# A second layer turned token-major for one half of the tokens, and a shorter head

## The chip, the core and the metric

The kernel runs on one core of a Trainium2 chip. The metric is the time on the device of one execution, in microseconds. The core's engines are TensorE (PE), VectorE (DVE), ScalarE (ACT), GpSimd (POOL) and SyncE (SP, which here only issues DMAs). Each runs its own queue in order; they meet at semaphores.

## What is computed

1024 tokens of 256 features pass two blocks, each with a layer norm ahead of it and a residual behind it. In the first block each token belongs to one of 4 experts by its token id; an expert's gate, up and down matrices are all the same 256 x 256 matrix. The second block is a mixture of 16 experts of 96 features, 4 per token, and a shared expert.

```python
# block 1, for each expert e (Wg, Wu, Wd are all ctx_2048)
g = silu(einsum('bsd,fd->bsf', h, Wg[e]))
u = einsum('bsd,fd->bsf', h, Wu[e])
y = einsum('bsf,df->bsd', g * u, Wd[e])
out = where((expert_ids == e)[..., None], y, out)
# block 2
scores = sigmoid(x @ router_w.T);  top 4 of scores + e_bias, weights normalised
routed = sum_e combine[:, e] * ((silu(g) * u) @ down_e.T)
# around them
x = x + block1(layernorm(x), ids)
x = x + block2(layernorm(x))
```

## The kernel before

The tokens are two halves of 512 (`h` = 0, 1), in tiles of 128. Inside a block the data lie feature-major: 128 features on the partitions, 512 tokens along the row, two such blocks of features (`KC` = 2). Matrices and activations are split into a high part of reduced precision and a low remainder, and each product is three matmuls (high x high, low weight x high, high weight x low), so a 512-column result over 256 features is 6 matmuls.

Block 1 is eight "mixes", written out in `mixes` (L291): (layer, half, feature block). A mix computes its 128 features for all 4 experts into 4 PSUM banks (24 matmuls of 512 columns); ACT copies expert 0 (`first_z`), and DVE overwrites the tokens of experts 1 to 3 with predicated copies (`pick`, masks from `thresholds`). Behind a layer-1 mix ACT takes the silu (`silu_z`), DVE multiplies (`hidden_product`), the high part is cast (`hidden_high` on ACT or `hidden_cast` on DVE), and DVE subtracts for the low part (`hidden_low`). Behind a layer-2 mix DVE adds the residual in `xt` (`add_block_1`), which gives x1. Six PSUM banks form a ring over the mixes (`ring_order`).

The layer norm wants tokens on the partitions. For half 0 of block 2, PE turns x1 (`x1_transposes`, 8 transposes of 128 x 128, in the midst of mix 5), DVE takes the statistics (`tile_stats(2)`, `layer_norm_vars(2)`), POOL the power -0.5 (`rstd_of`), DVE and ACT normalise two tiles each (`layer_norm_apply`, `apply_norm`), and PE turns the result back (`norm_transposes("n2", ...)`, behind the first 12 matmuls of mix 6). For half 1 of block 2 the turning goes over DVE's 32 x 32 transposes and DRAM (`turn_x1`, `write_x1`, `read_x1`, `turn_xn`, `write_xn`, `read_xn`), beside the second block's steps.

At the head, the tokens of half 0 are only centred ahead of the matmuls (tiles 0 and 2 on DVE by `centre`, 1 and 3 on ACT), and the deviation is multiplied in later as a row (`scale`, from `rstd_all`, which goes through DRAM). POOL subtracts for the low parts of the weights (`low_part(n)`, one per piece) and takes the powers. PE starts with 8 warm matmuls on zeros and has one more (256 columns) between the first and second pair of transposes (`first_transposes`).

Block 2 is a list of 26 steps (`items`): gate and up matmuls, then DVE's `product` with the router's weights (a row spread over the partitions by DMA, `spread_rows` on SP), `hidden_2`, a cast on ACT, `hid_low` on DVE, and two steps later the down matmuls.

The orders of all queues are written out by hand at the end of each engine's block: POOL's L480 to L497, ACT's L601 to L653, DVE's L874 to L964, PE's L1159 to L1184, SP's L370 to L454.

Of the kernel before, what the change touches and what calls it, by code (L numbers as in the profile page):

```python
# [61 lines left out]
XN_TURN, XN_WRITE, XN_READ = 6, 10, 11  # L62
SPREADS = 4
# [16 lines left out]
def build(nc, first_d, x_d, xt_d, ids_d, ctx_d, bias_d, gu_d, wd0_d, wd_d, out_d):  # L80
# [4 lines left out]
    with ExitStack() as ctx:  # L85
# [3 lines left out]
        def sem(name):  # L89
# [6 lines left out]
        xt = sb("xt", [P, KC, TOKENS])  # L96
        stage = sb("stage", [P, SLOTS, STAGE])
# [18 lines left out]
        power = sb("power", [P, TT])  # L116
# [27 lines left out]
        x1_d = nc.dram_tensor("x1_d", (HALF, D), F32, kind="Internal").ap()  # L144
        xn_d = nc.dram_tensor("xn_d", (QUARTERS, KC, LANES, HALF), F32, kind="Internal").ap()
# [26 lines left out]
        side_done, first_turned = sem("side_done"), sem("first_turned")  # L172
        xhi_done, xlo_done = sem("xhi_done"), sem("xlo_done")
# [17 lines left out]
                      ("x1", 0, 0, 4), ("x1", 0, 1, 5), ("n2", 0, 0, 4), ("n2", 0, 1, 5)]  # L191
        side_at = {u[:3]: n for n, u in enumerate(side_order)}

        def wait_side_read(eng, b, n):

            before = [u for u in side_order[:n] if u[3] == b]
            if not before:
                eng.wait_ge(pair_low, 1)
                eng.wait_ge(xlo_done, KC)
                return  # L200
            what, h, k, _ = before[-1]
            if what in ("n1", "n2"):
                count = (HALVES * KC if what == "n2" else 0) + h * KC + k + 1
                eng.wait_ge(xhi_done, max(count, KC))
                eng.wait_ge(xlo_done, count)
            else:
                eng.wait_ge(normed_v, (HALVES + 1) * TT // 2)
                eng.wait_ge(normed_a, (HALVES + 1) * TT // 2)

        ring_order = [("z", n, e) for n in range(7) for e in range(E1)]  # L210
        ring_order += [("gate", 0, 0), ("up", 0, 0)] + [("z", 7, e) for e in range(E1)]
# [5 lines left out]
        def wait_ring_read(eng, what, n, e):  # L217
# [7 lines left out]
            elif what == "z":  # L225
                eng.wait_ge(z_picked, n * (E1 - 1) + e)

# [14 lines left out]
        def wait_features(eng, what, h, k):  # L242
# [3 lines left out]
            else:  # L246
                eng.wait_ge(side_done, side_at[what, h, k] + 1)

# [42 lines left out]
        mixes = [(1, 0, 0), (1, 0, 1), (1, 1, 0), (2, 0, 0), (2, 0, 1), (1, 1, 1), (2, 1, 0), (2, 1, 1)]  # L291
        mixed = {mix: n for n, mix in enumerate(mixes)}

        def wait_mixed(eng, n):

            layer, h, m = mixes[n]
            eng.wait_ge(h1_done if layer == 1 else x1_done, h * KC + m + 1)
# [47 lines left out]
        def tile_to_norm(n, t):  # L345

            if n != HALVES:
                return x[:, n % HALVES * TT + t]
            at = t % (TT // KC) * D
            return side_bank("x1", 0, t // (TT // KC))[:, at:at + D]  # L350
# [10 lines left out]
        def _(sp):  # L361
# [15 lines left out]
            sp.dma_start(xt[:], xt_d).then_inc(xt_in, 16)  # L377
# [45 lines left out]

            def spread_rows(g):
# [10 lines left out]
            for g in range(1, N):  # L435
# [13 lines left out]
                if g == XN_READ:  # L449
                    read_xn()  # L450
                if g == place[1, SPREADS]:
# [5 lines left out]
        def _(pool):  # L457
# [16 lines left out]

            def rstd_of(n):

                pool.wait_ge(varied, n + 1)
                nc.gpsimd.tensor_tensor(deviation[:, 0:TT] if n == 0 else rstd[:, n], vareps[:, n], power[:], ALU.pow).then_inc(powered, 1)
# [21 lines left out]
        def _(act):  # L500
# [23 lines left out]

            def centre(t):
# [7 lines left out]
            def apply_norm(n):  # L533
# [4 lines left out]
                else:  # L538
                    act.wait_ge(side_done, side_at[("n1", 1, 1) if n == HALVES else ("n2", 0, 1)] + 1)
                for t in range(TT):  # L540
                    if t not in BY_VECTOR[n]:
                        nc.scalar.activation(xn[:, t], tile_to_norm(n, t), ACT.Identity, bias=shift[:, n, t:t + 1],
                                             scale=rstd[:, n, t:t + 1]).then_inc(normed_a, 1)

            def hidden_high(b):
                act.wait_ge(h1_product, b + 1)
                nc.scalar.activation(h_hi[:, b], hid[:, b % 2], ACT.Copy).then_inc(h1_high, 1)
# [678 lines left out]
```

## Time and profile before

| | us |
|---|---|
| median of 3 runs | 169.66 (169.48 to 169.74) |
| the profiled execution | 169.34 |
| its span in the trace | 167.2 |
| PE busy (share of the span) | 162.5 (97%) |
| DVE busy | 114.5 (68%) |
| ACT busy | 68.7 (41%) |
| POOL busy | 37.2 (22%) |

The span runs from the first to the last recorded event; the rest of the execution's time lies around it. Busy times of PE come from pipelined matmuls, so a matmul's own duration (0.395 us for 512 columns) is longer than the distance from one to the next. The chain of work that ended last is 95% PE: 23% of the span in `mix` (L1030), 41% in the gate and up matmuls, 21% in the down matmuls. A line of the timeline gives start, duration, engine, line, operation, output and inputs, a count where several were merged, and in brackets the idle time before it and what ended that.

### The profile page before, as it was taken

To read this page: it belongs to the slowest core of one execution; us is meant where nothing else is said; L and a number is where in the kernel's file an instruction comes from. 1 tells how busy PE (TensorE), PEld (TensorE's weight loads), DVE (VectorE), ACT (ScalarE), POOL (GpSimd) and SP (SyncE) were. 2 spreads that over 40 slices of the span, in tenths; PEclk is the share of its full clock that TensorE was granted. 3 is DMA by queue.
4 is the path that set the end of the run, shared out by engine and by line. 5 is a ranking of instruction groups with operands and counts; after the bars stand their busy time and mean duration, and the time that the engine had idled before them with its cause. 6 is when DMAs were issued, how large, how long until landed. Compare 5 with 4: busy or idle time off the path is not lost.

```text
span 167.2 us, 2186 instructions
## 1 busy us (share of the span) xinstructions
PE 162.5 (97%) x705; PEld 128.9 (77%) x705; DVE 114.5 (68%) x237; ACT 68.7 (41%) x116; POOL 37.2 (22%) x36
## 2 busy tenths in 40 slices
PE   7999999999999999999999999999999999999992
PEld 2788888888778888888888878888888888888880
DVE  1889999666957998779986744967714444444462
ACT  3654342831359134536734538452222222222210
POOL 1384000656241045556970000000000000000000
PEclk9999999999999999999999999999999999999999
DMA  5891380164304065987225400025441112200003
GB/s 172 275 408 44 107 291 0 21 206 161 115 4 127 16 205 192 219 240 211 67 61 163 153 0 4 1 103 165 173 141 67 63 63 63 65 0 0 4 0 125
DMA packets 12199, 18.78 MB, mean 112 GB/s; under 512 B 3772, under 2 KB 6044, under 8 KB 12060
## 3 DMA queue, kind: packets, MB, share of 16 engines
q1 hardware_dynamic: 12188, 18.64, 34.9%
q8 instruction: 6, 0.10, 0.2%
q14 instruction: 5, 0.04, 0.1%
HBM read 16.39 MB, written 2.24 MB: 111 GB/s over the span
## 4 chain that ended last, share of the span: by engine, by line
PE 95%; DMA 2%; DVE 1%; DVEq 0%; issue 0%
PE bank L1030 23%; PE bank L1131 15%; PE bank L1129 13%; PE bank L1130 13%; PE bank L1149 7%; PE bank L1152 7%; PE bank L1150 7%; DMA first<-first_d 2%; PE bank L998 1%; PE bank L1071 1%; PE bank L1065 1%; PE bank L1126 1%; PE bank L1125 1%; PE bank L987 1%; PE bank L1078 1%; PE bank L1060 1%
## 5 line engine op out<-in xcount | busy, mean ns | idle before, releaser
L1131 PE MATMUL bank<-xn_lo,gu_hi 128*128 128x512 f32 (+1 forms) x104 | 41.1, 395 | 0.0
L1129 PE MATMUL bank<-xn_hi,gu_lo 128*128 128x512 f32 x96 | 38.0, 396 | 0.0
L1130 PE MATMUL bank<-xn_hi,gu_hi 128*128 128x512 f32 x96 | 38.0, 396 | 0.0
L599 ACT ACTIVATE h_hi<-hid 128x512 fp32r<-128x512 f32 (+1 forms) x26 | 16.4, 632 | 45.6 <-DVE hid L860 45.6
L865 DVE TENSOR_TENSOR h_lo<-hid,h_hi 128x512 fp32r<-128x512 f32 (+1 forms) x26 | 18.0, 691 | 14.9 <-ACT h_hi L599 14.9
L1131 PEld LDWEIGHTS bank<-xn_lo,gu_hi 128*128 128x128 f32 (+1 forms) x104 | 19.4, 187 | 4.9
L589 ACT ACTIVATE act_sb<-bank 128x512 f32<-128x512 f32 (+1 forms) x26 | 15.4, 592 | 17.5 <-PE bank L1131 17.4
L472 POOL TENSOR_TENSOR gu_lo<-stage,gu_hi 128x512 fp32r<-128x512 f32 x12 | 17.2, 1457 | 21.7 <-ACT gu_hi L504 16.3
L1129 PEld LDWEIGHTS bank<-xn_hi,gu_lo 128*128 128x128 f32 x96 | 18.0, 188 | 4.4
L1130 PEld LDWEIGHTS bank<-xn_hi,gu_hi 128*128 128x128 f32 x96 | 18.0, 188 | 4.3
L749 DVE COPY_PREDICATED prod<-beyond,bank 128x512 f32<-128x512 uint8 x24 | 17.6, 737 | 5.1 <-PE bank L1030 4.4
L1149 PE MATMUL bank<-h_hi,wd_lo 128*128 128x512 f32 (+1 forms) x52 | 20.6, 396 | 0.0
L1150 PE MATMUL bank<-h_hi,wd_hi 128*128 128x512 f32 (+1 forms) x52 | 20.6, 395 | 0.0
L1152 PE MATMUL bank<-h_lo,wd_hi 128*128 128x512 f32 (+1 forms) x52 | 20.5, 395 | 0.0
L860 DVE TENSOR_TENSOR hid<-prod,bank 128x512 f32<-128x512 f32 x24 | 16.5, 688 | 2.0
L847 DVE TENSOR_TENSOR prod<-act_sb,ids 128x512 f32<-128x512 f32 x12 | 9.6, 796 | 8.6 <-ACT act_sb L589 8.6
L847 DVE TENSOR_TENSOR prod<-act_sb,first 128x512 f32<-128x512 f32 x12 | 10.0, 832 | 6.3 <-ACT act_sb L589 5.7
L1030 PE MATMUL bank<-h_hi,ctx_hi 128*128 128x512 f32 x32 | 12.7, 398 | 0.0
L1030 PE MATMUL bank<-h_lo,ctx_hi 128*128 128x512 f32 x32 | 12.7, 395 | 0.0
L1030 PE MATMUL bank<-h_hi,ctx_lo 128*128 128x512 f32 x32 | 12.7, 395 | 0.0
L1152 PEld LDWEIGHTS bank<-h_lo,wd_hi 128*128 128x128 f32 (+1 forms) x52 | 9.8, 188 | 2.4
L1150 PEld LDWEIGHTS bank<-h_hi,wd_hi 128*128 128x128 f32 (+1 forms) x52 | 9.8, 188 | 2.3
(102 smaller groups left out, 213.2 us busy)
## 6 DMA issues: line engine op xcount, KB each, us to landing
stage<-gu_d SPq DMA_DIRECT2D x6, 512.0 KB, 3.9
stage<-wd_d SPq DMA_DIRECT2D x3, 512.0 KB, 4.3
first<-comb_d SPq DMA_DIRECT2D x8, 192.0 KB, 2.9
ids<-comb_d SPq DMA_DIRECT2D x8, 192.0 KB, 3.3
stage<-ctx_d SPq DMA_DIRECT2D x4, 256.0 KB, 6.0
xt<-xt_d SPq DMA_DIRECT2D x1, 1024.0 KB, 9.9
first<-comb_d SPq DMA_DIRECT2D x8, 128.0 KB, 3.0
ids<-comb_d SPq DMA_DIRECT2D x8, 128.0 KB, 2.9
```

The lines of the kernel that those rows point to most:

```text
L472: ins = nc.gpsimd.tensor_tensor(lo[:, s], st[:, s], hi[:, s].bitcast(F32), ALU.subtract)
L749: nc.vector.copy_predicated(prod[:, n % 2], beyond[:, e - 1, h * HALF:(h + 1) * HALF], ring_bank("z", n, e)[:]).then_inc(z_picked, 1)
L847: nc.vector.tensor_tensor(prod[:, g % 2], act_sb[:, g % 2], rows, ALU.mult).then_inc(prod_done, 1)
L860: nc.vector.tensor_tensor(hid[0:w, g % 2], src, up_bank(g)[0:w, :], ALU.mult).then_inc(hid_done, 1)
L865: nc.vector.tensor_tensor(h_lo[0:w, slot[g]], hid[0:w, g % 2], h_hi[0:w, slot[g]].bitcast(F32), ALU.subtract).then_inc(hlo_done, 1)
L1030: return nc.tensor.matmul(ring_bank("z", n, e)[:], (ctx_hi, ctx_lo)[a][:, m, e, k], parts[k][b], start=start, stop=stop)
L1129: nc.tensor.matmul(out[:], gu_lo[:, cols], xn_hi[:, h, k], start=(k == 0), stop=False)
L1130: nc.tensor.matmul(out[:], gu_hi[:, cols], xn_hi[:, h, k], start=False, stop=False)
L1131: ins = nc.tensor.matmul(out[0:rows, :], gu_hi[:, wide], xn_lo[:, h, k], start=False, stop=(k == KC - 1))
L1149: nc.tensor.matmul(acc[k][:], wd_lo[0:w, c, cols], hi, start=(c == 0), stop=False)
L1150: nc.tensor.matmul(acc[k][:], wd_hi[0:w, c, cols], hi, start=False, stop=False)
L1152: ins = nc.tensor.matmul(acc[k][:], wd_hi[0:w, c, cols], lo, start=False, stop=(c == ITEMS - 1))
```

## The change

- Half 0's second layer is computed with tokens on the partitions (`row_mix`): the stationary operand is a block of 128 tokens of the hidden activations, the moving operand the matrices of a pair of experts, 512 columns. So x1 of half 0 comes out token-major in `x1_rows`. `x1_transposes`, its two entries of `side_order` and the mixes (2, 0, 0) and (2, 0, 1) go; the list of mixes has six entries now, and the order is mixes 0, 1, 2, the rows, 3, 4, 5.
- ACT copies expert 0's columns (`row_z`, 256 per tile), DVE picks experts 1 to 3 in operations of 256 columns with a mask of one byte per token (`row_thresholds`, `pick_rows`), adds the residual (`add_rows`), and takes the statistics from there.
- The tokens of a tile are dealt out in runs of 32 (`hidden` writes them so), and "n2"'s transposes undo that with a strided output.
- x1 of half 0 is needed feature-major for the last residual: DVE's transposes behind steps 8 and 9 (`turn_x0`), DMAs behind 12 and 13 of SP's loop (`write_x0`, `read_x0`), and `output(0)` waits for them.
- POOL waits for the four row adds (instead of x1) ahead of `low_part(7)` and `rstd_of(2)`. `layer_norm_apply(2)` lies ahead of the last pick of mix 3.
- At the head DVE's `centre` sums and subtracts (`tensor_reduce`, `scalar_tensor_tensor`) in place of `bn_stats`, `bn_aggr` and a subtraction; all four tiles' statistics come later. The warm matmul between the pairs goes. One power of 8 columns stands for two of 4, ahead of `low_part(3)` rather than behind it, and waits for the second half's variances.
- The residual is loaded in two halves, half 0 token-major, and the ids of half 0 once more by tokens.

```diff
-        mixes = [(1, 0, 0), (1, 0, 1), (1, 1, 0), (2, 0, 0), (2, 0, 1), (1, 1, 1), (2, 1, 0), (2, 1, 1)]
+        mixes = [(1, 0, 0), (1, 0, 1), (1, 1, 0), (1, 1, 1), (2, 1, 0), (2, 1, 1)]
...
+        def hidden(tile, b, at):
+            if b >= KC:
+                return tile[:, at]
+            order = "p (b t j) -> p b t j" if tile is hid else "p (t b j) -> p b t j"
+            return tile[:, at].rearrange(order, t=TT, j=LANES)
...
+            def first_deviations():
+                pool.wait_ge(varied, HALVES)
+                nc.gpsimd.tensor_tensor(deviation[:, 0:HALVES * TT], vareps[:, 0:HALVES].rearrange("p n t -> p (n t)"),
+                                        power[:], ALU.pow).then_inc(powered, HALVES)
...
-            for n in range(E1):
+            for n in range(E1 - 1):
                 low_part(n)
-            rstd_of(0)
-            rstd_of(1)
+            first_deviations()
+            low_part(E1 - 1)
             for n in range(E1, E1 + 3):
                 low_part(n)
-            pool.wait_ge(x1_done, KC)
+            pool.wait_ge(row_added, TT)
             low_part(E1 + 3)
             rstd_of(2)
...
             first_z(2)
-            first_z(3)
+            row_z(0)
             silu_z(2)
             hidden_high(2)
+            row_z(1)
             high_part(4)
             high_part(5)
+            row_z(2)
             high_part(6)
-            first_z(4)
+            row_z(3)
             high_part(7)
             high_part(8)
             router_low_rows()
-            first_z(5)
-            silu_z(5)
+            first_z(3)
             apply_norm(2)
+            silu_z(3)
...
             def centre(t):
                 dve.wait_ge(x_in[t // (TT // 2)], 16)
-                tile_stats(0, t)
+                step(nc.vector.tensor_reduce(minus_mean[:, t:t + 1], x[:, t], AX.X, ALU.add))
                 dve.wait_ge(dstep, steps[0])
-                step(nc.vector.bn_aggr(meanvar[:, 0, t], stats[:, t]))
-                dve.wait_ge(dstep, steps[0])
-                nc.vector.tensor_scalar(xn[:, t], x[:, t], meanvar[:, 0, t, 0:1], None, ALU.subtract).then_inc(normed_v, 1)
+                nc.vector.scalar_tensor_tensor(out=xn[:, t], in0=minus_mean[:, t:t + 1].to_broadcast([P, D]), scalar=-1.0 / D, in1=x[:, t],
+                                               op0=ALU.mult, op1=ALU.add).then_inc(normed_v, 1)
...
+            def pick_rows(t, experts=range(1, E1)):
+                dve.wait_ge(row_first, t + 1)
+                dve.wait_ge(rows_masked, E1 - 1)
+                for e in experts:
+                    dve.wait_ge(row_done, 2 * t + e // 2 + 1)
+                    if e > 1:
+                        dve.wait_ge(row_picked, t * (E1 - 1) + e - 1)
+                    z = ring_bank("rows", t, e // 2)[:, e % 2 * D:(e % 2 + 1) * D]
+                    nc.vector.copy_predicated(x1_rows[:, t], beyond_rows[:, e - 1, t:t + 1].to_broadcast([P, D]),
+                                              z).then_inc(row_picked, 1)
+            def add_rows(t):
+                dve.wait_ge(row_picked, (t + 1) * (E1 - 1))
+                dve.wait_ge(x_rows_in, 16)
+                residual = xt[:, t * D // HALF, t * D % HALF:][:, 0:D]
+                nc.vector.tensor_tensor(x1_rows[:, t], x1_rows[:, t], residual, ALU.add).then_inc(row_added, 1)
...
             masked.append(thresholds(1))
+            row_thresholds()
             pick(2, masked[1])
-            pick(3, masked[0], [1])
+            pick_rows(0, [1])
             hidden_product(2)
-            pick(3, masked[0], [2])
+            pick_rows(0, [2])
             hidden_low(2)
-            pick(3, masked[0], [3])
-            add_block_1(3)
-            pick(4, masked[0])
+            pick_rows(0, [3])
+            add_rows(0)
+            for t in range(1, TT):
+                tile_stats(2, t - 1)
+                pick_rows(t)
+                add_rows(t)
+            tile_stats(2, TT - 1)
+            layer_norm_vars(2)
+            pick(3, masked[1], [1, 2])
+            layer_norm_apply(2)
+            pick(3, masked[1], [3])
+            hidden_product(3)
+            hidden_cast(3)
+            hidden_low(3)
+            x_low("n2", 0, 0)
+            x_low("n2", 0, 1)
...
-                for t, warm_steps in enumerate((0, 0, 1, 0)):
-                    keep_warm(warm_steps, HALF // 2)
+                for t in range(TT):
                     wait_normed(pe, 0, t)
...
+            def row_mix():
+                hi, lo = ([w[:, b].rearrange("p (t c) -> p t c", c=P) for b in range(KC)] for w in (h_hi, h_lo))
+                def moving(w, pair, k):
+                    return w[:, :, 2 * pair:2 * pair + 2, k].rearrange("p m e f -> p e m f")
+                for t in range(TT):
+                    for pair in range(2):
+                        wait_ring_read(pe, "rows", t, pair)
+                        out = ring_bank("rows", t, pair)[:].rearrange("p (e m f) -> p e m f", e=2, m=KC)
+                        for k in range(KC):
+                            if t == 0 and pair == 0:
+                                pe.wait_ge(h1_high, k + 1)
+                            nc.tensor.matmul(out, hi[k][:, t], moving(ctx_hi, pair, k), start=(k == 0), stop=False)
+                            nc.tensor.matmul(out, hi[k][:, t], moving(ctx_lo, pair, k), start=False, stop=False)
+                            if t == 0 and pair == 0:
+                                pe.wait_ge(h1_done, k + 1)
+                            ins = nc.tensor.matmul(out, lo[k][:, t], moving(ctx_hi, pair, k), start=False, stop=(k == KC - 1))
+                        ins.then_inc(row_done, 1)
...
             mix(1, {1: lambda: norm_transposes("n1", 1, 1)})
-            for n in range(2, 5):
-                mix(n)
-            mix(5, {1: lambda: (x1_transposes(0, 0), x1_transposes(0, 1))})
-            mix(6, features=[0])
+            mix(2)
+            row_mix()
+            mix(3)
+            mix(4, features=[0])
             norm_transposes("n2", 2, 0)
-            mix(6, experts=[0, 1], features=[1])
+            mix(4, experts=[0, 1], features=[1])
             gate_or_up(0, False)
             gate_or_up(0, True)
```

## Rows read from the trace of the kernel before

**Rows 1.** The page, busy time, share of the span and instructions of each engine.
```profile
PE 162.5 (97%) x705; PEld 128.9 (77%) x705; DVE 114.5 (68%) x237; ACT 68.7 (41%) x116; POOL 37.2 (22%) x36
```

**Rows 2.** What PE waited for: us in total, times, longest.
```profile
PE bank L977 <- DVE warm L874: 1.2, 1, 1.2
PE bank L998 <- DVE xn L687: 0.3, 1, 0.3
```

**Rows 3.** The chain that ended last: start (end of the one before), us, work.
```profile
6.12 0.21 PE bank L977
...
16.67 22.39 PE bank L1030 x96
39.06 0.87 PE bank L1010 x8
...
45.53 0.87 PE bank L987 x8
```

**Rows 4.** Timeline of DVE: second variances, first norm, mixes 2 and 5, second block.
```profile
12.50 0.17 DVE L678 TENSOR_SCALAR vareps<-meanvar 128x4 f32<-128x4 f32 x1
...
14.59 0.16 DVE L713 SCALAR_TENSOR_TENSOR shift<-meanvar,rstd 128x4 f32<-128x4 f32 x1
14.67 0.73 DVE L721 TENSOR_SCALAR xn<-first,meanvar,rstd 128x256 f32<-128x256 f32 x2
...
25.56 3.19 DVE L749 COPY_PREDICATED prod<-beyond,bank 128x512 f32<-128x512 uint8 x4
28.69 0.69 DVE L757 TENSOR_TENSOR hid<-act_sb,prod 128x512 f32<-128x512 f32 x1
...
45.09 0.43 DVE L763 TENSOR_SCALAR h_hi<-hid 128x512 fp32r<-128x512 f32 x1
...
60.86 1.61 DVE L847 TENSOR_TENSOR prod<-act_sb,first 128x512 f32<-128x512 f32 x1 [0.18 <-DMA first<-comb_d]
```

**Rows 5.** Groups of DVE by form: busy us, mean ns; idle before, releaser.
```profile
L749 DVE COPY_PREDICATED prod<-beyond,bank 128x512 f32<-128x512 uint8 x24 | 17.6, 737 | 5.1 <-PE bank L1030 4.4
L865 DVE TENSOR_TENSOR h_lo<-hid,h_hi 128x512 fp32r<-128x512 f32 x24 | 16.6, 691 | 14.7 <-ACT h_hi L599 14.7
...
L670 DVE BATCH_NORM_STATS2 stats<-first 128x6 f32<-128x256 f32 x12 | 4.4, 416 | 3.3 <-DMA first<-first_d 2.7 <-DMA first<-x_d 0.5
...
L872 DVE TENSOR_TENSOR xt<-bank,xt 128x256 f32<-128x256 f32 x2 | 0.8, 420 | 0.7 <-PE bank L1152 0.7
```

**Rows 6.** Timeline of ACT: first norm, the cast of mix 2, the first late weights.
```profile
14.79 1.09 ACT L542 ACTIVATE xn<-first,shift,rstd 128x256 f32<-128x256 f32 x2 [4.30 <-DVE shift L713]
...
29.41 0.63 ACT L547 ACTIVATE h_hi<-hid 128x512 fp32r<-128x512 f32 x1 [0.76 <-DVE hid L757]
29.95 1.51 ACT L504 ACTIVATE gu_hi<-stage 128x448 fp32r<-128x448 f32 x2
```

**Rows 7.** Timeline of POOL: a memset, the first powers, low parts of the weights.
```profile
0.73 0.10 POOL L458 MEMSET power<- 128x4 f32 x1 [0.29 <-POOLq L1219]
...
12.55 1.18 POOL L478 TENSOR_TENSOR deviation<-vareps,power 128x4 f32<-128x4 f32 x1
13.53 1.03 POOL L478 TENSOR_TENSOR rstd<-vareps,power 128x4 f32<-128x4 f32 x1
30.59 1.22 POOL L468 TENSOR_TENSOR gu_lo<-stage,gu_hi 128x448 fp32r<-128x448 f32 x1 [16.03 <-ACT gu_hi L504]
31.77 3.05 POOL L472 TENSOR_TENSOR gu_lo<-stage,gu_hi 128x512 fp32r<-128x512 f32 x2
...
37.91 2.54 POOL L472 TENSOR_TENSOR wd_lo<-stage,wd_hi 128x512 fp32r<-128x512 f32 x2 [2.38 <-DVE xt L777]
...
60.63 2.99 POOL L472 TENSOR_TENSOR gu_lo<-stage,gu_hi 128x512 fp32r<-128x512 f32 x2 [9.75 <-ACT gu_hi L504]
```

**Rows 8.** Timeline of PE: the transposes of the two norms.
```profile
15.64 1.03 PE L987 MATMUL bank<-first,xn 128*128 128x128 f32 x8
...
45.37 1.04 PE L987 MATMUL bank<-first,xn 128*128 128x128 f32 x8
```

More of the change, by code:

```diff
@@ L201, in wait_side_read @@
             what, h, k, _ = before[-1]
[L202 to L211, printed above, removed]
+            count = (HALVES * KC if what == "n2" else 0) + h * KC + k + 1
+            eng.wait_ge(xhi_done, max(count, KC))
+            eng.wait_ge(xlo_done, count)
+        ring_order = [("z", n, e) for n in range(3) for e in range(E1)]
+        ring_order += [("rows", t, pair) for t in range(TT) for pair in range(2)]
+        ring_order += [("z", n, e) for n in (3, 4) for e in range(E1)]
+        ring_order += [("gate", 0, 0), ("up", 0, 0)] + [("z", 5, e) for e in range(E1)]
         ring_at = {u: n for n, u in enumerate(ring_order)}
@@ L226, in wait_ring_read @@
                 eng.wait_ge(z_picked, n * (E1 - 1) + e)
+            elif what == "rows" and e == 0:
+                eng.wait_ge(row_first, n + 1)
+                eng.wait_ge(row_picked, n * (E1 - 1) + 1)
+            elif what == "rows":
+                eng.wait_ge(row_picked, (n + 1) * (E1 - 1))
         def side_bank(what, h, c):
@@ L422, in read_xn, with write_x0, read_x0 @@
                     sp.dma_start(xn_turn[q * LANES:(q + 1) * LANES], rows[q]).then_inc(xn_back, 16)
+            def write_x0():
+                sp.wait_ge(x0_turned, TT)
+                rows = turn_d.rearrange("q k i (b c) -> b i (q k) c", c=P)
+                blocks = x[:, TT:].rearrange("p t d -> p (t d)").rearrange("p (m c) -> p m c", c=P)
+                for b in range(QUARTERS):
+                    sp.dma_start(rows[b], blocks[b * LANES:(b + 1) * LANES]).then_inc(x0_out, 16)
+            def read_x0():
+                sp.wait_ge(x0_out, QUARTERS * 16)
+                rows = turn_d.rearrange("q k i n -> q i k n")
+                for q in range(QUARTERS):
+                    sp.dma_start(xt[q * LANES:(q + 1) * LANES, :, 0:HALF], rows[q]).then_inc(x0_back, 16)
             def spread_rows(g):
@@ L450, in _ @@
                     read_xn()
+                if g == X0_WRITE:
+                    write_x0()
+                if g == X0_READ:
+                    read_x0()
                 if g == place[1, SPREADS]:
@@ L523, in first_z, with row_z @@
                 nc.scalar.activation(prod[:, n % 2], ring_bank("z", n, 0)[:], ACT.Copy).then_inc(z_first, 1)
+            def row_z(t):
+                act.wait_ge(row_done, 2 * t + 1)
+                nc.scalar.activation(x1_rows[:, t], ring_bank("rows", t, 0)[:, 0:D], ACT.Copy).then_inc(row_first, 1)
             def centre(t):
@@ L768, in hidden_low @@
                 dve.wait_ge(h1_high, b + 1)
-                nc.vector.tensor_tensor(h_lo[:, b], hid[:, b % 2], h_hi[:, b].bitcast(F32),
+                nc.vector.tensor_tensor(hidden(h_lo, b, b), hidden(hid, b, b % 2), hidden(h_hi, b, b).bitcast(F32),
                                         ALU.subtract).then_inc(h1_done, 1)
```

129 lines of the change are left out of this document (73 added, 56 removed).

## The prediction

> **What bounds the kernel now.** I read the page's busy times first, then what TensorE (PE) waits for, then the chain of work that ended last, and only then the other engines' timelines around the two places that the diff touches. PE is busy for 162.5 of 167.2 us [rows 1], and its waits come to 1.5 us in all, both in the first 5 us [rows 2]. So from there on PE never waits, and the time is PE's own instruction stream. Its pace is read from the chain: 96 matmuls of 512 columns in 22.39 us, 0.233 us each [rows 3]. Two things follow. A PE instruction taken out behind the head gives back its full price. And a new PE wait is paid in full too, since nothing behind it has slack to give back. The question is whether the other engines still deliver in time.
>
> **What PE loses and gains.** `x1_transposes` goes: 8 transposes in 0.87 us [rows 3], so -0.87 us. `row_mix` has 4 token tiles x 2 pairs of experts x 2 feature halves x 3 terms = 48 matmuls of 512 columns; the two mixes that it replaces had 2 x 4 x 2 x 3 = 48. I take the same 0.233 us. Its moving operand is four runs of 128 columns instead of one of 512, and the "n2" transposes write runs of 32; no row shows either. At 2% more on the 48 it would be +0.2 us; a gain is excluded, since as many columns stream. I take 0.
>
> **The new chain behind the rows.** Most of the forecast hangs on it. All times are in the clock of the trace before.
> PE: mix 1 has 12 matmuls left at 16.67 and mix 2 has 24, so the rows start at 16.67 + 36 x 0.233 = 25.07 and end at 25.07 + 11.2 = 36.27; mix 3 (half 1, layer 1, feature 1) ends at 41.87, the first 12 of mix 4 at 44.67, the 8 "n2" transposes at 45.54. That is 0.87 us ahead of before, as it must be (45.53 + 0.87 there [rows 3]). The next matmul needs `h_hi` of mix 3's block, the third needs `h_lo`.
> DVE: 512 elements of a tensor_tensor take 0.69 [rows 4], 256 take 0.42, a pick of 512 takes 0.737 [rows 5]. A pick of 256 is not in the trace; it lies between half of 0.737 (0.37) and 0.737. The step of 0.27 us that separates the two tensor_tensors gives 0.47, and I take that. Four picks in a row take 3.19 us [rows 4], so one that waits for the one before it starts 0.1 us after its end: 0.57 per pick. A tile is three picks (1.71), an add (0.42) and its stats (0.42 [rows 5], of which some 0.07 overlaps): 2.5 us. PE makes one each 2.8 us, so DVE would keep up, but it starts behind. Three thresholds of 4 elements come first (0.1 each, the 0.17 us of such an instruction [rows 4] overlapped), so mix 2's picks start at 25.86 instead of 25.56 and everything behind them is 0.3 us later: product at 28.99 for 28.69, its cast on ScalarE (ACT) at 29.71 for 29.41 [rows 6], `h_lo` 30.41 to 31.08. Tile 0's first two picks fill the gaps in which DVE waits for ACT; the third ends at 31.47 and the add wants to start at 31.57.
> POOL then stands in the way. ACT is 0.3 us later and has one row copy (0.3) ahead of its 448-wide cast, which goes from 29.95 [rows 6] to 30.55. POOL's 1.22 us subtraction came 0.64 us behind that cast's start [rows 7]: now 31.2 to 32.4. An operation of DVE with two inputs in SBUF waits for a POOL operation that runs: the product at 60.86 took 1.61 us instead of 0.69 [rows 4] beside a POOL subtraction that began at 60.63 [rows 7]. So add 0 ends at about 32.7, not 32.0. POOL's two halves of 512 follow, 1.3 us each once DVE lets go, until 35.1; add 1, wanted at 34.76, ends at 35.4. Tiles 2 and 3 have no such company: add 2 ends at 37.9, add 3 at 40.4.
> POOL waits for that last add (`row_added`, 4), and then has `low_part(7)`, 2.54 us [rows 7], and the power, 1.03, in that order: 40.48 + 2.54 + 1.03 = 44.05. (`low_part(7)` began at 37.91 before.) `layer_norm_apply(2)` stands in DVE's queue ahead of the last pick of mix 3. From the power to the end of its two tiles are 0.8 us (14.56 to 15.40 in the other norm [rows 4, 7]), so that pick starts at 44.86, although its matmuls ended at 41.87. Queued behind it is the rest of that block's path: pick 0.74, silu 0.63, product 0.69, cast 0.43, with 0.03 between [rows 4 to 6]: `h_hi` at 47.45, `h_lo` at 48.2. PE had issued its transposes by 45.37 + 0.87 before [rows 8], and has by 45.4 now; it stands until 47.5, 2.2 us, and 0.3 us more at `h_lo`. The new wait is +2.5 us.
> Its bounds: without POOL's company the last add is 1.0 us earlier, and at 0.37 per pick some 11 picks on the path give 1.1: 0.4 us is left. With the variances and a strided cast of layer 1 held up too (0.2 and 0.3 us) it is 3.0.
> The page "VectorE: DVE Perf Modes" of the Trainium skill, section "The TRN2 errata", speaks against just this part: each small operation pays a fixed latency, and it advises 512 elements or more. Its formula for PSUM sources gives 0.39 us for a pick of 256, an estimate; by it the wait would be 0.9 us shorter. For 512 it gives 0.66, below the 0.737 of the row here.
>
> **The head.** Out go a `bn_aggr` on DVE with its wait and one warm matmul (0.21 us [rows 3]) between the pairs. DVE's first tile may come 0.2 us earlier, and PE up to 0.4. That doesn't last to 16.4: the "n1" transposes need ACT's second tile of half 1, done at 15.88 (14.79 + 1.09 [rows 6]), and PE's last two stood at about 16.24 (8 from 15.64 on [rows 8]), 0.3 us in hand. That tile hangs on the power, and now one power of 8 columns stands for two of 4. It can't start before the second variances (12.50 + 0.17 [rows 4]). Bounds: 1.03 us as for 4, and 2.0 for two of them [rows 7]. A POOL memset of 4 columns took 0.10 us and a subtraction of 448 took 1.22 [rows 7], so a microsecond for 4 columns isn't the price of an instruction; it goes by columns, and I take 1.85. It ends at 14.55, where the second one ended before (14.56). But the shift came 0.86 us behind the first power (13.73 to 14.59 [rows 4, 7]), with the turn of the deviations and a pick between, and now these come behind the one power: shift at 15.41, ACT's tile at 16.7, PE's last two transposes at 16.75 instead of 16.24. That is +0.5 us, whatever the head gained. At 1.03 the tile comes 0.14 us later than before, and 0.1 of the gain stays: -0.1. `low_part(3)`, now behind the power, ends by 15.9, ahead of its matmuls behind 16.4. The row of deviations is 0.8 us later as well, and with it DVE's layer 1 by some 0.65 where PE is 0.5 later: +0.15 on the wait above.
>
> **What costs nothing.** `turn_x0` moves 1024 columns, as much as two 512-wide operations, 1.4 us in two portions; DVE waits 0.6 us for ACT's cast in each of 24 steps (14.7 us [rows 5]) and has its results ready a step ahead of PE. `write_x0` on SP waits for the second portion, and behind it stand the spread rows of step 13, which are needed four steps later; `read_x0` lies ahead of the router rows of half 1, for which SP stands anyway. Without that cover it would be the 1.4 us once. Two halves of a load move the same bytes as the one.
>
> **Sum.** -0.87 + 0.5 + 2.5 + 0.15 = +2.3 us. The profiled execution took 169.34 us (span 167.2 and 2.1 around it), so 171.6; the median of the runs is 0.3 us above the profiled one: 169.66 + 2.3 = 171.9.
>
> **Rivals.** (1) DVE keeps pace: if its picks are short and POOL's subtractions miss the adds, the last add is done by 38.0, the power by 41.7, and PE finds `h_hi` ready. For it: 2.5 us per tile are below PE's 2.8. Against: DVE begins the rows 3 us behind. Then only transposes and head count, -0.87 with -0.1 to +0.5: 168.7 to 169.3. It decides from 2.4 us less on DVE's path. Chance 0.17. (2) Half of it: a wait near 0.9 us that eats the transposes' gain, 169.3 to 170.0; 0.10. (3) The wait as worked out, 170.0 to 173.0; 0.65. (4) The idle stretch costs PE its clock: in the head a step of 256 columns took 0.21 us [rows 3], the lower level (1.2 GHz), when PE had only begun to work. Ten matmuls at half pace behind the wait would be 2 us more, 173.5 to 174. Before has no such stretch, so only that row speaks for it; 0.08. The page "TensorE: Matmul & The Clock Gate" of the skill, Part 1, has the clock fall after idling; no run here shows that in mid-kernel yet. That the change doesn't do what it says is left out: the transposes are gone from PE's queue.
>
> **Chances.** What a measurement can tell from no change is 0.2% (0.34 us). Faster: rival 1 nearly whole, 0.17. Same: the low half of rival 2, 0.07. Slower: 0.76. The range 169.1 to 173.2 leaves out most of rivals 1 and 4.
>
> **What would show it.** In the profile after: no line of x1 transposes; among PE's waits 2 to 3 us for DVE's `h_hi` or `h_lo` of mix 3; POOL's second power done near 44 to 45 us, with DVE waiting for it ahead of the last pick of mix 3; a DVE add of rows over 1 us. At the head a power of 1.8 us, and PE waiting for ACT's tile near 16. A power of 1.0 us and no PE wait near 46 would prove me wrong.

## The result, and the profile after

The changed kernel took 171.94 us as the median of six runs (171.21 to 173.22); the kernel before took 169.45 us beside it (169.24 to 169.74). The ratio is 1.015 with an interval of [1.011, 1.019]: slower by 1.5%, 2.5 us, close to the 171.9 us that was forecast. In the two longest runs (172.91 and 173.22 us) TensorE's granted clock was 0.99 over the run, in the other four 1.00 (171.21 to 172.03, median 171.64); experiment 9 comes back to that.

The profiled run took 171.86 us (span 169.7) against 169.34 (167.2), so there are 2.52 us to account for. First, what PE waited for (us in total, times, longest), against [rows 2]:

```profile
PE bank L1140 <- DVE h_hi L856: 1.5, 1, 1.5
PE bank L1076 <- DVE warm L969: 1.2, 1, 1.2
PE bank L1089 <- DVE xn L778: 1.1, 1, 1.1
PE bank L1098 <- DVE xn L743: 0.2, 1, 0.2
```

Two waits are new. The second line of before, for the first norm's tiles, has lost 0.1 us; `warm` is as it was. PE's timeline places the new ones (start, us, work, idle time before it and what ended it):

```profile
16.85 1.15 PE L1089 MATMUL bank<-first,xn 128*128 128x128 f32 x8 [1.15 <-DVE xn L778]
17.75 0.48 PE L1140 MATMUL bank<-xn_hi,ctx_hi 128*128 128x512 f32 x1
...
26.23 0.40 PE L1117 MATMUL bank<-ctx_hi,h_hi 128*128 128x512 f32 x1
...
37.43 0.40 PE L1140 MATMUL bank<-xn_hi,ctx_hi 128*128 128x512 f32 x1
...
45.83 1.04 PE L1089 MATMUL bank<-first,xn 128*128 128x128 f32 x8
48.40 0.50 PE L1140 MATMUL bank<-h_hi,ctx_hi 128*128 128x512 f32 x1 [1.54 <-DVE h_hi L856]
48.73 0.39 PE L1140 MATMUL bank<-h_hi,ctx_lo 128*128 128x512 f32 x1
49.12 0.50 PE L1140 MATMUL bank<-h_lo,ctx_hi 128*128 128x512 f32 x1
...
50.16 0.39 PE L1235 MATMUL bank<-xn_hi,gu_hi 128*128 128x512 f32 x1
```

Read with the same instructions of before, these lines are the whole account. The mixing resumes at 17.75 behind the "n1" transposes, at 16.43 in before (the first row of the next fence): the head costs +1.32. The "n2" transposes start at 45.83, at 45.37 before [rows 8]: of the 1.32 the missing transposes of x1 have given back 0.86. The router's first matmul starts at 50.16 instead of 47.64 (the second row), 2.52 late: from the transposes on another 2.06 us is lost, nearly all of it in front of `h_hi` and then, 0.16 us (48.73 to 49.12 instead of one step of 0.233), in front of `h_lo`. So -0.87 + 1.32 + 2.06 = +2.51 of 2.52 us. And the 48 matmuls of the token-major mix run from 26.23 to 37.43: 0.233 us each, the pace of [rows 3]. The two rows of PE's timeline in before that answer:

```profile
16.43 0.48 PE L1030 MATMUL bank<-xn_hi,ctx_hi 128*128 128x512 f32 x1
...
47.64 0.40 PE L1125 MATMUL bank<-xn_hi,gu_hi 128*128 128x512 f32 x1
```

The chain of work that ended last (start, us, work) shows the wait behind the rows as one thread of single steps:

```profile
40.97 0.44 DVE x_rows L833
...
41.47 1.41 POOL wd_lo L512 x2
42.88 1.10 issue
43.98 1.03 POOL rstd L524
...
45.83 0.67 DVE prod L806
...
46.53 0.64 ACT act_sb L617
...
47.19 0.70 DVE hid L850
...
47.91 0.44 DVE h_hi L856
```

Last add of the rows, POOL's low part of a weight (2.54 us with the "issue" behind it), the power, the norm, then the last pick of mix 3, silu, product and cast. The pick depends on none of that; it is only queued behind the norm.

### The profile page after: what moved, and what is told of

The parts are those of the page before. It is cut to its first block, busy times and chain, and to the rows that moved or that the text cites. A ratio compares the mean times of both kernels' runs of the same rounds, so it can differ in the third digit from the quotient of the medians.

```text
span 169.7 us, 2207 instructions
## 1 busy us (share of the span) xinstructions
PE 162.3 (96%) x696; PEld 127.9 (75%) x696; DVE 119.4 (70%) x258; ACT 69.0 (41%) x118; POOL 36.7 (22%) x35
## 4 chain that ended last, share of the span: by engine, by line
PE 70%; DVE 8%; issue 2%; POOL 1%; ACT 1%; DVEq 0%
PE bank L1241 14%; PE bank L1239 13%; PE bank L1240 13%; PE bank L1259 7%; PE bank L1260 7%; PE bank L1262 7%; PE bank L1140 5%; DVE x_rows L825 3%; DVE prod L806 2%; DVE x_rows L833 2%; PE bank L1236 1%; PE bank L1235 1%; DVE hid L850 1%; POOL wd_lo L512 1%; ACT act_sb L617 1%
## 5 line engine op out<-in xcount | busy, mean ns | idle before, releaser
L806 DVE COPY_PREDICATED prod<-beyond,bank 128x512 f32<-128x512 uint8 x18 | 13.1, 733 | 1.2 <-PE bank L1140 0.7
L1259 PEld LDWEIGHTS bank<-h_hi,wd_lo 128*128 128x128 f32 (+1 forms) x52 | 9.8, 188 | 2.3
L1140 PE MATMUL bank<-xn_hi,ctx_hi 128*128 128x512 f32 x24 | 9.6, 399 | 0.0
L1140 PE MATMUL bank<-xn_lo,ctx_hi 128*128 128x512 f32 x24 | 9.5, 396 | 0.0
```

What stands on the lines that cost most here:

```text
L806: nc.vector.copy_predicated(prod[:, n % 2], beyond[:, e - 1, h * HALF:(h + 1) * HALF], ring_bank("z", n, e)[:]).then_inc(z_picked, 1)
L1140: return nc.tensor.matmul(ring_bank("z", n, e)[:], (ctx_hi, ctx_lo)[a][:, m, e, k], parts[k][b], start=start, stop=stop)
L1259: nc.tensor.matmul(acc[k][:], wd_lo[0:w, c, cols], hi, start=(c == 0), stop=False)
```

## Experiments

The whole has three suspects: the head, the order on POOL and DVE behind the rows, and DVE's late start into the rows. The first two runs split the change; the next four take one suspect each; the last six put the results together and look into the granted clock.

**1 and 2. Half of the change each.** One kernel is before with the head's edits alone:

```diff
+                step(nc.vector.tensor_reduce(minus_mean[:, t:t + 1], x[:, t], AX.X, ALU.add))
...
-            rstd_of(0)
-            rstd_of(1)
+            first_deviations()
+            low_part(E1 - 1)
...
-                    keep_warm(warm_steps, HALF // 2)
```

The other is after with the head of before (the same lines the other way round, and two powers of 4 columns).

> The kernel before with the head's edits alone (sum and subtraction for DVE's centring, no warm matmul, statistics of all four tiles, one power for both halves ahead of low_part(3)); layer 2 stays as before. Theory: the trace after has PE's second set of 8 transposes end 1.33 us later than before, and nothing behind it has slack, so this kernel takes 169.45 + 1.3 = 170.8 us, with a PE wait of about 1.1 us at those transposes and none near 46 us. Rival: the late power is hidden in the kernel before by PE's other work, and the time stays within 0.3 us of 169.45.

> The changed kernel with the whole head of before (DVE's centring by bn_stats, the warm matmul, two powers behind low_part(3)). Theory: PE gains its 0.87 us, and the wait for h_hi and h_lo of mix 3 stays, a little shorter since DVE wins 1.6 us from the head and PE 1.3: 2.06 - 0.3 = 1.75 us; 169.45 - 0.87 + 1.75 = 170.3 us. Rival: the head's delay and the wait behind the rows overlap (whoever comes late at the head waits less there), and the time stays near 171.9.

Measured: head alone 170.15 us, ratio 1.0057 [1.0038, 1.0076]; rows alone 170.46, 1.0072 [1.0046, 1.0099]. Each half makes the kernel slower by itself, by 0.86 and 1.17 us against the 169.29 us of before beside them; together that is 2.0, where after lies 2.5 above before, and its four runs at full clock 2.2. The rows come out as expected; one of their nine runs, 171.99 us, had a granted clock of 0.99. Their profile has the one wait and none at the "n1" transposes (PE's waits, rows alone):

```profile
PE bank L1142 <- DVE h_hi L857: 1.6, 1, 1.6
```

The head's median is 0.65 us below what was expected. Its nine runs lie in two groups, five at 169.88 to 170.15 and four at 170.60 to 170.86. The profiled one, 170.6, is of the upper group and shows the price of +1.3 (PE's waits and timeline of DVE, head alone):

```profile
PE bank L995 <- DVE xn L729: 1.1, 1, 1.1
```

```profile
11.20 1.41 DVE L679 BATCH_NORM_STATS2 stats<-first 128x6 f32<-128x256 f32 x4 [0.77 <-DMA first<-x_d]
```

Half 1's statistics wait for their tokens' load, and all later steps with them, since the one power needs the second variances. With two powers half 0's turn goes ahead; with one it shares the late start. The profile of run 3, which has the same head, shows it with the tokens there in time (DVE, then PE):

```profile
10.35 1.39 DVE L726 BATCH_NORM_STATS2 stats<-first 128x6 f32<-128x256 f32 x4
```

```profile
15.92 1.15 PE L1087 MATMUL bank<-first,xn 128*128 128x128 f32 x8 [0.24 <-DVE xn L776]
```

The statistics start 0.85 us earlier and PE waits 0.24 us at the "n1" transposes instead of 1.1. So the lower group is likely that of an early load; no run of it was profiled, so for run 1 that is argued, not shown.

**3. The power ahead of the weight.** After, with POOL's order behind the rows changed:

```diff
-            pool.wait_ge(row_added, TT)
-            low_part(E1 + 3)
             rstd_of(2)
             pool.wait_ge(xlo_done, (HALVES + 1) * KC)
-            for n in range(E1 + 4, early_pieces + 4):
+            for n in range(E1 + 3, early_pieces + 4):
```

> The changed kernel with POOL's third power directly behind the variances and low_part(7) moved behind the wait for xlo_done. Theory: the power ends near 43.5 us instead of 45.0, DVE's first two picks of mix 3 then become the limit, the last pick starts 0.8 us earlier, and PE's wait falls from 2.06 to about 1.25: 171.1 us. Rival: DVE's own work behind the rows sets the wait and the power is beside it: no change from 171.9.

Measured 170.8 us (170.38 to 171.25), 1.0094 [1.0065, 1.0123]: 1.1 us of the 2.5 come back, or 0.8 against after's four runs at full clock. What PE waited for there:

```profile
PE bank L1138 <- DVE h_hi L854: 0.4, 1, 0.4
...
PE bank L1138 <- DVE prod L804: 0.3, 1, 0.3
```

The wait for `h_hi` is down from 1.5 to 0.4 us, and a new one for a pick has come, further on: the low part that was moved away now runs beside the router's chain. The two together are 0.8 us less. (The profiled run, 170.38 us, gained 0.9 more at the head, as shown above; that is not this edit's.)

**4. The pick ahead of the norm.** After, with DVE's and ACT's order changed instead:

```diff
-            pick(3, masked[1], [1, 2])
-            layer_norm_apply(2)
-            pick(3, masked[1], [3])
+            pick(3, masked[1])
             hidden_product(3)
+            layer_norm_apply(2)
             hidden_cast(3)
```

> The changed kernel with the last pick and hidden_product of mix 3 ahead of layer_norm_apply(2) on DVE, and silu_z(3) ahead of apply_norm(2) on ACT. Rival first: if the place in the queue behind the power is the whole cost, h_hi is ready 2 us earlier and the time falls to about 170.0. Theory: DVE leaves the rows so late that the norm's tiles then come at 47 us and PE waits for them at its transposes instead, about 1.5 us: 171.4 us.

Measured 170.89 us, 1.0088 [1.0064, 1.0111], between the theory's 171.4 and the rival's 170.0, and 0.7 us better than after's runs at full clock. It had no wait for `h_hi` at all, but the wait had moved (timeline of PE):

```profile
46.88 1.15 PE L1088 MATMUL bank<-first,xn 128*128 128x128 f32 x8 [1.08 <-DVE xn L778]
```

The norm itself is late, so whichever goes first, the other is waited for. Reordering DVE wins only a part of what POOL's order costs; runs 3 and 4 agree that the power behind `low_part(7)` is what comes late.

**5. Two powers again.** After, with the head's powers split (`first_deviations` replaced by `rstd_of(0)` and `rstd_of(1)` behind all four low parts).

> The changed kernel with two powers of 4 columns behind low_part(3), as before, and the other edits of the head kept. Theory: what is late at the head is the one power, which waits for the second half's variances, takes 1.68 us, and has DVE's turn, pick and a shift held up by low_part(3) behind it. With two, the shift comes 1.2 us earlier, PE's wait at the n1 transposes goes, and the time falls by about 1.1 us against the changed kernel, to 1.4 us above the kernel before (170.7). Rival: the four tiles' statistics ahead of the second half's make the variances late, and two powers change little (within 0.4 us).

Median 172.21 us, 1.0143 [1.0105, 1.0181], against 170.7 expected. The run with a granted clock of 1.0 took 170.41 and had no wait at the "n1" transposes; the other three, 172.09 to 172.38, had 0.99, and they make the median. At full clock the expectation holds within 0.3 us, on one run; the other three weren't profiled.

**6. The thresholds on POOL.** After, with `thresholds(1)` and `row_thresholds()` taken from DVE's queue ahead of the rows and given to POOL, idle there.

```diff
-            masked.append(thresholds(1))
-            row_thresholds()
...
+                nc.gpsimd.tensor_scalar(beyond_rows[:, e - 1], id_rows[:], float(e * PER_EXPERT), None,
+                                        ALU.is_ge).then_inc(rows_masked, 1)
```

> The changed kernel with half 1's thresholds and the row thresholds taken from DVE to POOL (idle from 16.4 to 32.5 us). Theory: PE's wait for h_hi comes from DVE's work between layer 1 and the last row add; 1.3 us less of it move the last add by as much and cut the wait from 2.06 to about 0.85 us: 1.2 us faster than the changed kernel (170.7). Rival: DVE's tiles are paced by PE's row tiles or by POOL's subtractions, so an earlier start is lost there, and the time stays within 0.4 us.

Measured 170.84 us, 1.0086 [1.0070, 1.0102]. The wait for `h_hi` is 0.6 us where after has 1.5: of the 1.3 us of thresholds ahead of the rows on DVE, 0.9 come out of the wait. So the wait has two parts, POOL's order (run 3) and DVE's late start.

**7 and 8. All three undone.** The head of before, the power early and the thresholds on POOL (7); the same with after's centring by a sum, without the warm matmul, and two powers (8).

> The changed kernel with the whole head of before, POOL's third power directly behind the variances (low_part(7) later), and the masks made on POOL. Theory: the last row add is done by 38.1 us, the power by 40.1, h_hi by 44.6, ahead of PE's need at 45.4; no PE wait is left, only the 0.87 us of transposes is gone: 168.5 us, 0.8 below the kernel before (169.3). Rival: another wait takes its place (the deviations, POOL's later low parts), and it stays at or above 169.3.

> As e7_all_three, but with the changed kernel's centring by a sum, its four tiles of statistics and no warm matmul between the pairs; two powers. Theory: the shorter head starts PE's matmuls by at most 0.1 to 0.3 us earlier and the n1 transposes take most of that back: 168.3 to 168.6 us. Rival: the longer statistics make the second variances late by what the arrival of the second half's tokens leaves, and it is 0.3 us or more slower than e7_all_three.

169.92 us, 1.0035 [1.0012, 1.0059], and 169.78, 1.0029 [1.0009, 1.0050]: the two heads, with their different centring, can't be told apart. The wait for `h_hi` was gone in both profiles, and yet some 1.3 us of the expected gain was missing. Two waits of run 8 cover that (PE's waits, then DVE's timeline):

```profile
PE bank L1197 <- ACT ctx_hi L557: 0.9, 1, 0.9
PE bank L1149 <- DVE prod L816: 0.8, 1, 0.8
```

```profile
51.64 1.34 DVE L910 TENSOR_TENSOR biased<-scores,bias 128x64 f32<-128x64 f32 x1
```

The biased score, two small inputs in SBUF, took 0.21 us in before and 1.34 here, beside a POOL low part that began at 50.36. The pick behind it is late, and PE stands 0.8 us for it; run 7's profile has the same (1.36 us and 0.8). The other wait is in the head, for the first context piece; it is in run 7's profile too (0.8), but not in after's. In both ACT waited for the piece's load; why that came late stays open.

**9. The new loads later.** After, with the two new loads issued behind the read of the scales:

```diff
-            sp.dma_start(id_rows[:], id_rows_d).then_inc(id_rows_in, 16)
-            sp.dma_start(xt[:, :, 0:HALF], x_rows_d).then_inc(x_rows_in, 16)
...
             sp.dma_start(rstd_all[:], ...).then_inc(rstd_in, 16)
+            sp.dma_start(id_rows[:], id_rows_d).then_inc(id_rows_in, 16)
+            sp.dma_start(xt[:, :, 0:HALF], x_rows_d).then_inc(x_rows_in, 16)
             sp.wait_ge(rstd_in, 16)
```

> The changed kernel, with one thing moved: the two new loads (the ids token-major, x token-major) are issued behind the read of half 0's scales (17.4 us in the changed kernel's trace), not in the stretch in which the first context pieces and half 1's tokens arrive (5.9 and 6.8 us there). Nothing needs them before 27 us. Theory: the small packets of the new loads are what makes the first pieces and half 1's tokens arrive at different times, and what brings the runs at a granted clock of 0.99 that the kernel before does not have; without them no run is at 0.99, half 1's statistics start by 10.7 us instead of 11.28, and the median is 171.2 to 171.5 (the best of the changed kernel's runs was 171.21). Rival: the loads stand behind the others in the queue and take nothing from them; the runs spread over 171.2 to 173.2 as before and some are at 0.99.

171.64 us (170.77 to 173.07), 1.0147 [1.0107, 1.0186], two of six runs at 0.99, as the rival had it: the theory falls, the loads are not what lowers the clock. But this time a run with 0.99 was the profiled one, 173.07 us, and it shows where the clock goes. PE's timeline, and then a stretch of it (busy time of each engine, granted clock, DMA share, GB/s):

```profile
48.03 0.50 PE L1140 MATMUL bank<-h_hi,ctx_hi 128*128 128x512 f32 x1 [1.55 <-DVE h_hi L856]
...
49.80 0.59 PE L1235 MATMUL bank<-xn_hi,gu_hi 128*128 128x512 f32 x1
...
53.44 0.39 PE L1235 MATMUL bank<-xn_hi,gu_hi 128*96 128x512 f32 x1
```

```profile
49.80:53.10 3.30, 3.30 (x9) 2.34 (x8) 0.83 (x2) 0.63 (x3) 2.51 (x2) 0.50 0.02 5
```

After the wait PE works six matmuls and then takes 3.64 us (49.80 to 53.44) for nine, which at 0.233 are 2.10, with a granted clock of 0.50 (the lower level, 1.2 GHz): 1.5 us more. 3.3 us at 0.50 lower the mean over the span of 170.9 us by 0.01, which is the 0.99 of the whole run. The four runs at 1.00 lie 1.3 to 2.3 us below this one. Run 7's profile has the same in its head, behind waits of 0.5 and 0.8 us: granted clock 0.50 from 8 to 10 us, 0.66 to 12. But waits as long left the clock at 1.00 in the profiles of after (1.54), run 2 (1.57), runs 10 and 11 (1.33) and run 8 (0.93 in the head). Runs at 0.99 (0.986 to 0.99) occur only in kernels with new waits: 2 of 6 of after and of run 9, 3 of 4 of run 5, 1 of 9 of run 2, 2 of 12 of run 7, 1 of 12 of run 8, and none of the kernel before's; runs 3, 4, 6 and 10 wait anew too and have none. So the new wait costs its own length in every run, and in some 1.5 us more go to the clock; that the wait brings the fall on is argued from this order, not shown.

**10 to 12. Where low part 7 goes.** Run 7 with POOL's `low_part(7)` right behind the power (10); that with the loads of 9 (11); that with one wait more (12):

```diff
             rstd_of(2)
+            pool.wait_ge(h1_done, RING)
             low_part(E1 + 3)
             pool.wait_ge(xlo_done, (HALVES + 1) * KC)
```

> The run with all three undone parts (e7) with one thing more: POOL's low part 7 stands right behind the third power, not behind the wait for the second norm's low parts. In e7 and e8 that late place put POOL's low parts 7 and 8 beside the router's chain on DVE (the biased score took 1.34 us instead of 0.21), and TensorE waited 0.8 us for a pick. Theory: that wait goes, and nothing comes in its place, since DVE between the power and the hidden product has one small step of two SBUF inputs (the shift, 0.14 us), and the high part of mix 3 had 0.6 us to spare: 169.9 - 0.8 = 169.1. Rival: POOL now holds up the shift or the hidden product by as much as 1.3 us, which uses up the 0.6 us and gives 0.5 us back as a wait for the high part of mix 3: 169.6 to 169.9, no better than e7.

> Both of the runs before at once: all three parts undone, low part 7 right behind the power, the new loads behind the read of the scales. If the two are independent and the loads cost the head what e7's profile showed (0.8 us of TensorE waiting for the first context piece), 168.3 to 168.8, some 0.4 to 0.7% faster than the kernel before and with no run at a granted clock of 0.99; this is the changed kernel's idea with its three costs taken away, of which the 0.87 us for four transposes of x1 is what should be left. If the loads cost nothing, the same as e10.

> The last run (e11) with one thing moved: POOL's low part 7 waits until mix 3's hidden block has its low part, behind the third power. In e10's and e11's profiles it ran from 41.0 to 43.6 us (41.7 to 44.2), beside DVE's shift (0.98 us instead of 0.14) and norm (1.79 instead of 0.73 for two), and TensorE waited 1.3 us for the high part of mix 3; in their quick runs, some 1.3 us below the others, DVE's steps presumably came first. Theory: now it runs at some 45.8 to 48.4 us, where DVE has the low parts of the second norm (one input from PSUM) and a pick, and POOL's low part 8 ends where it did in the kernel before; no wait for the high part, none for a pick, all runs in the quick group: 168.8 to 169.3, 0.1 to 0.4% below the kernel before. Rival: DVE's low parts are held up in place of the shift, the router's products come up to 1 us late: 169.6 to 170.2, in one group.

Run 10: 170.12 us, 1.003 [1.0006, 1.0055]; run 11: 170.11, 1.0014 [0.9986, 1.0041]. Neither reaches its theory (169.1, and 168.3 to 168.8), and run 11 is no faster than run 10: where the loads stand is worth nothing here. Both split into two groups, 10 into five runs at 169.03 to 169.42 and seven at 169.96 to 170.75, 11 into five at 168.79 to 169.36 and six at 169.97 to 171.03. The profiled ones are of the upper groups, and there the rival had come about (DVE and POOL of run 10):

```profile
41.34 0.98 DVE L779 SCALAR_TENSOR_TENSOR shift<-meanvar,rstd 128x4 f32<-128x4 f32 x1
42.24 1.79 DVE L787 TENSOR_SCALAR xn<-x_rows,meanvar,rstd 128x256 f32<-128x256 f32 x2
```

```profile
41.01 2.54 POOL L513 TENSOR_TENSOR wd_lo<-stage,wd_hi 128x512 fp32r<-128x512 f32 x2
```

The shift and the norm, 0.16 and 0.73 us without company, wait for the low part, and `h_hi` is waited for again, 1.3 us. No run of a lower group was profiled, so what they do differently isn't shown. Run 12 puts the low part into a stretch in which DVE has nothing that it holds up: **168.60 us, ratio 0.9955 [0.9939, 0.9971]**, just below the 168.8 to 169.3 expected, all twelve runs from 167.97 to 169.21. It beats both kernels. PE's waits, and the same lines of DVE and POOL:

```profile
PE bank L1088 <- DVE warm L982: 1.2, 1, 1.2
PE bank L1101 <- DVE xn L788: 0.4, 1, 0.4
PE bank L1111 <- DVE xn L754: 0.2, 1, 0.2
```

```profile
41.89 0.15 DVE L780 SCALAR_TENSOR_TENSOR shift<-meanvar,rstd 128x4 f32<-128x4 f32 x1
41.96 0.74 DVE L788 TENSOR_SCALAR xn<-x_rows,meanvar,rstd 128x256 f32<-128x256 f32 x2
...
44.77 0.43 DVE L869 TENSOR_SCALAR h_hi<-hid 128x512 fp32r<-128x512 f32 x1
```

```profile
40.56 1.04 POOL L525 TENSOR_TENSOR rstd<-vareps,power 128x4 f32<-128x4 f32 x1 [5.32 <-DVE vareps L745]
...
46.01 2.55 POOL L513 TENSOR_TENSOR wd_lo<-stage,wd_hi 128x512 fp32r<-128x512 f32 x2 [4.41 <-DVE h_lo L875]
```

`h_hi` is there at 45.2, before PE asks, and no wait stands behind the head. Of the 0.87 us of transposes 0.7 are left.

## Why the prediction was right, step by step

**Transposes: -0.87, exact.** No line of them is left, and the "n2" transposes moved ahead by that against the head's delay. Run 12 confirms it: behind its head no wait eats the gain, and its profiled run lies 0.43 us below that of before (168.91 against 169.34) although its "n1" transposes wait 0.4 us that before doesn't have.

**48 matmuls for 48, at no extra: exact,** 11.20 us. Four runs of 128 columns in the moving operand cost nothing here.

**The wait behind the rows: 2.65 forecast, 2.06 measured, by the mechanism named.** The chain above is the one that was worked out, link by link. What was mis-sized is DVE's path ahead of it. In the clock of before (DVE's head is 1.64 us later in after) the last add ended at 39.76, not at 40.4, 0.64 early; the head's delay of DVE over PE, 0.32 us (1.64 against 1.32) where 0.15 was added, took 0.17 of that back. A pick of 256 from PSUM takes 0.43 to 0.45 us where 0.47 was taken from two neighbouring rows; three in a row take 1.54, not 1.71. The page "VectorE: DVE Perf Modes" of the Trainium skill, section "The TRN2 errata", would have 0.39, an estimate by its formula; the rows lie between. POOL's company came as forecast: add 0 took 1.12 us and add 1 0.72 instead of 0.42 (DVE's timeline, then POOL's):

```profile
32.84 1.12 DVE L833 TENSOR_TENSOR x_rows<-x_rows,xt 128x256 f32<-128x256 f32 x1
...
34.34 1.55 DVE L825 COPY_PREDICATED x_rows<-beyond_rows,bank 128x256 f32<-128x256 uint8 x3
35.92 0.72 DVE L833 TENSOR_TENSOR x_rows<-x_rows,xt 128x256 f32<-128x256 f32 x1
```

```profile
32.52 1.16 POOL L508 TENSOR_TENSOR gu_lo<-stage,gu_hi 128x448 fp32r<-128x448 f32 x1 [16.16 <-ACT gu_hi L550]
33.64 2.72 POOL L512 TENSOR_TENSOR gu_lo<-stage,gu_hi 128x512 fp32r<-128x512 f32 x2
```

The picks between them have the same company and are as short as elsewhere.

**The head: +0.5 forecast, +1.32 measured.** This is the step that failed in size. The direction and the link (one power for both halves, then the turn, a pick and the shift behind it) were right, and the power of 8 columns took 1.68 us, 1.85 having been taken. What was missing stands in DVE's and POOL's timelines of after:

```profile
10.17 1.20 DVE L736 TENSOR_SCALAR vareps<-meanvar 128x4 f32<-128x4 f32 x1
...
13.12 0.17 DVE L736 TENSOR_SCALAR vareps<-meanvar 128x4 f32<-128x4 f32 x1
...
15.90 0.48 DVE L770 SCALAR_TENSOR_TENSOR shift<-meanvar,deviation 128x4 f32<-128x4 f32 x1
```

```profile
8.79 2.56 POOL L508 TENSOR_TENSOR ctx_lo<-stage,ctx_hi 128x512 fp32r<-128x512 f32 x2 [0.87 <-ACT ctx_hi L550]
13.44 1.68 POOL L518 TENSOR_TENSOR deviation<-vareps,power 128x8 f32<-128x8 f32 x1 [2.09 <-DVE vareps L736]
15.09 1.28 POOL L508 TENSOR_TENSOR ctx_lo<-stage,ctx_hi 128x512 fp32r<-128x512 f32 x1
```

The prediction took the second variances at 12.50, as in before; they came at 13.12, 0.62 late. The first variances, 0.17 us by themselves, were held for 1.20 by POOL's low parts, and half 1's statistics are queued behind them. The start of those statistics sets the head's price: in the six profiles with the one power they start at 11.28 us (after), 11.20 (run 1), 11.06 (4), 11.03 (6), 10.88 (9) and 10.35 (3), and PE waits 1.15, 1.13, 0.98, 0.96, 0.94 and 0.24 us at the "n1" transposes; in runs 1, 4, 6 and 9 it is the tokens' load that holds them. And `low_part(3)`, set behind the power and costed only by when its matmuls need it, runs into the shift: 0.48 instead of 0.16. The prediction applied its rule on DVE beside POOL to the adds and forgot it ten lines later for the shift; and the rule, put for two inputs in SBUF, was too narrow, since the variances have one.

**The sum** was 2.3 against 2.5, with -0.6 on one term and +0.8 on the other: that the time came out better than its parts is luck.

**What was to cost nothing did:** `write_x0` went out at 98.08 us and `read_x0` at 101.96, and PE has no wait there.

**The rivals.** Rival 1 (DVE keeps pace) needed 2.4 us off DVE's path and was priced at 168.7 to 169.3. Run 12 takes 2.5 us of low part and 1.3 of thresholds off it, has the head of before, and lies just below that: the price was right, the condition not met. Rival 4 (the clock) was given 2 us and 0.08. Its mechanism exists: run 9's profile has nine matmuls at the lower level behind the wait, 1.5 us, and the two runs of after at 0.99 lie 1.4 us above the mean of its other four (172.91 and 173.22 against 171.21 to 172.03); those two weren't profiled. It sits on top of the likeliest case in some runs and lifted after's median by 0.3 us, from the 171.64 of the four at 1.00; without it the time would have been 171.6, not the 171.9 of the forecast. The row that the rival rested on does not show the granted clock: the step of 0.21 us is at the pace of 1.2 GHz, but the profile of before gives 1.00 for that stretch (6.12 to 6.33 us). The page "TensorE: Matmul & The Clock Gate" of the Trainium skill, Part 1, has the clock fall after idling. Run 9's profile agrees in mid-kernel, behind 1.55 us of waiting; after's, with 1.54, kept 1.00.

**The signs to look for** came: no line of x1 transposes, a wait for `h_hi`, an add over 1 us, a power of 1.68, the third power done at 45.0 with DVE waiting for it. Only the head's wait is put down to DVE's tile of the norm, the first that PE needs, not to ACT's.

## To carry to other kernels

When the bound engine never waits, an instruction taken from it is worth its price only if every queue that delivers to it still keeps its order: here 0.87 us was bought with a longer path on DVE and POOL, and the wait that this made cost 2.06. Ask of each engine's queue what stands ahead of the next thing that is needed but doesn't depend on it; with the head as it was, the thresholds on POOL, the third power right behind its variances and one weight's low part placed where DVE has nothing for it to hold up (run 12), the same idea gains 0.45%. And a step that is merged with a later one (one power for two halves) inherits the lateness of the later one's inputs.

## What the runs showed of the hardware

- DVE steps held while POOL ran were not only those with two large inputs: the variances, 4 columns from SBUF, took 1.20 us instead of 0.17 (after), the norm's two tiles 1.79 instead of 0.73 (run 10). No pick from PSUM was held in these profiles.
- A POOL power took 1.01 to 1.39 us for 4 columns over the profiles and 1.68 for 8. Two in a row took 2.01 in before (12.55 to 14.56 us), so merging them saves 0.3 us of POOL, not one whole power.
- The thresholds of 512 ids took 0.37 us each on DVE and some 1.55 on POOL (three in 1.09, and in 4.63 to 4.75).
- Behind 1.55 us of waiting in mid-kernel PE ran nine matmuls at a granted clock of 0.50 (run 9); behind 1.54 (after) and 1.57 us (run 2) it kept 1.00. What decides stays open.
